# First mixer of a four-layer block: decay differences and key products written for GpSimd, and a new order on VectorE and ScalarE

## The reference

```python
xc = silu(causal_depthwise_conv(x))            # x: 16 sequences, 512 tokens, 256 wide
q, kg, v, g = xc @ wq, xc @ wkg, xc @ wv, xc @ wg + bg
gk = log_sigmoid(kg) / 16                      # decay of each key dimension
k = 1 - exp(gk)
# 8 heads, 16 key and 32 value dimensions each; over the tokens:
S = S * exp(gk_t)[..., None] + k_t[..., None] * v_t[..., None, :]
o_t = einsum('bhk,bhkv->bhv', q_t * scale, S)
o = o + sigmoid(einsum('bhld,hd,bhld->bhl', q, aug, k)[..., None] * v)
o = (o - mean(o)) * rsqrt(var(o) + eps)        # over a head's 32 values
x = layernorm(x + (silu(g) * o) @ wout)
```

## Time and profile before

| | us |
|---|---|
| three runs | 4456.34, 4467.64, 4469.37 |
| median | 4467.64 |
| profiled execution | 4455.1 |
| its span | 4453.5 |

### The profile page before, as it was taken

One profiled execution on the slowest core, in us unless ns is written; L12 is line 12 of the kernel. 1 busy time (PEld: TensorE's weight loads), 2 busy tenths in 40 slices (PEclk: granted clock), 3 DMA queues, 4 the chain that ended last, 5 costly groups with the idle time before them and its releaser, 6 DMA issues. The chain is left out here.

```text
span 4453.5 us, 69246 instructions
## 1 busy us (share of the span) xinstructions
PE 3941.6 (89%) x23860; PEld 3041.0 (68%) x23860; DVE 2464.7 (55%) x5456; ACT 1990.0 (45%) x4069; POOL 1195.6 (27%) x1878
## 2 busy tenths in 40 slices
PE   6888788598999999995689999989999999779998
PEld 3555555377888888884477777777777777656665
DVE  6888888452222222223667777777777777431111
ACT  5666665111222112221466666666666666432221
POOL 0111111101212221212344444444444443300000
PEclk8899899699999999997799999999999999889999
DMA  1010010254555555553111111111111111011111
GB/s 35 30 44 30 30 44 21 66 148 163 187 187 186 180 180 186 186 188 103 37 39 44 43 44 44 44 44 44 44 44 44 44 44 25 21 62 57 57 57 47
DMA packets 199445, 347.09 MB, mean 78 GB/s; under 512 B 75396, under 2 KB 150404, under 8 KB 180996
## 3 DMA queue, kind: packets, MB, share of 16 engines
q1 hardware_dynamic: 169284, 271.16, 18.8%
q0 software_dynamic: 29904, 72.65, 5.6%
HBM read 276.61 MB, written 68.16 MB: 77 GB/s over the span
## 5 line engine op out<-in xcount | busy, mean ns | idle before, releaser
L525 ACT ACTIVATE moe_rel<-moe_fc 128x512 f32<-128x512 f32 x284 | 169.6, 597 | 798.3 <-PE moe_fc L490 798.3
L490 PE MATMUL moe_fc<-moe_xT,moe_win 128*128 128x256 f32 x2272 | 503.6, 380 | 1.5 <-issue 0.8
L501 PE MATMUL moe_o<-moe_wout,moe_hT 128*128 128x256 f32 x2272 | 502.0, 379 | 0.0
L490 PEld LDWEIGHTS moe_fc<-moe_xT,moe_win 128*128 128x128 f32 x2272 | 432.6, 190 | 61.1 <-issue 2.1
L501 PEld LDWEIGHTS moe_o<-moe_wout,moe_hT 128*128 128x128 f32 x2272 | 426.3, 190 | 55.1
L549 DVE TENSOR_TENSOR moe_hT<-moe_rel 128x512 f32<-128x512 f32 x284 | 196.6, 692 | 360.7 <-ACT moe_rel L525 360.7
L1743 DVE SCALAR_TENSOR_TENSOR gdr_y<-gdr_bank,gdr_cw,gdr_y 128x511 f32<-128x511 f32 (+2 forms) x384 | 287.3, 748 | 41.4 <-ACT gdr_y L2053 27.0
L2330 PE MATMUL gdr_bank<-gdr_hT,gdr_wqkv 128*128 128x512 f32 x512 | 279.2, 678 | 29.6 <-ACT gdr_qk L2068 24.5
L558 DVE COPY moe_osb<-moe_o 128x512 f32<-128x512 f32 x71 | 49.1, 691 | 424.9 <-PE moe_o L501 424.9
L1305 PE MATMUL gdr_bank<-gdr_hT,gdr_wqkv 128*128 128x512 f32 x512 | 225.3, 598 | 3.6 <-ACT gdr_hT L1323 3.6
L1338 DVE TENSOR_TENSOR gdr_kb<-gdr_bank,gdr_x 128x512 f32<-128x512 f32 x32 | 20.6, 686 | 366.4 <-PE gdr_bank L1314 366.4
(11 more groups left out here) (393 smaller groups left out, 8804.2 us busy)
## 6 DMA issues: line engine op xcount, KB each, us to landing
moe_win<-in_moe_w SPq DMA_DIRECT2D x71, 1024.0 KB, 7.6
moe_wout<-in_moe_w SPq DMA_DIRECT2D x71, 1024.0 KB, 5.2
slots_out<-moe_osb POOLq DMA_DIRECT2D x71, 256.0 KB, 7.3
gdr_fz<-mixed_rows SPq DMA_DIRECT2D x18, 512.0 KB, 3.8
gla_xp<-in_xT_rows SPq DMA_DIRECT2D x16, 512.0 KB, 4.4
gla_xres<-in_x_rows SPq DMA_DIRECT2D x16, 512.0 KB, 3.8
token_rows<-gla_x POOLq DMA_DIRECT2D x16, 512.0 KB, 3.4
rt_W<-in_fc_b SPq DMA_DIRECT2D x32, 256.0 KB, 3.4
```

Of the source, the lines that this page charges most:

```text
L490: ins = nc.tensor.matmul(fc_ps[j][:, m % 2, :], win[u][:, c, m * P:(m + 1) * P], xT[:, c, :], start=(c == 0), stop=(c == DT - 1))
L501: ins = nc.tensor.matmul(o_ps[u][:, t, :], hT[u][:, k, t * P:(t + 1) * P], wout[u][:, k, :], start=(k == 0), stop=(k == FT - 1))
L525: nc.scalar.activation(rel[:, j, :, :], fc_ps[j][:], ACT.Relu).then_inc(relu_done, 1)
```

## The change

DVE no longer makes kt: GpSimd makes the eight differences as soon as G is there, ACT takes their exponentials as before, and GpSimd multiplies by k. GpSimd's loop gets the same `body` as the other engines: pow for rstd of b - 1, differences and products of b + 1, then the layer norm's pow and the two stores of b - 1. A new semaphore `Dk` counts GpSimd's differences, `G` the scan; the scan now waits until GpSimd has read the last G.

On DVE the calls of a body stand in a new order: variance and the product with gs (head norm 1 and 2) come first, `on` (3) ahead of the third masked scores, the gates behind them; the residual sum z (tail 0) comes right behind the fourth masked scores, the first convolution behind z and ahead of `products`; the layer norm's statistics, x1 and the logits are four parts now; the head means (0) are taken in the body that makes o. On ACT the squares move along to the end of the body, and the turned `on` is copied ahead of the exponentials. PE's and SP's code is unchanged.

```diff
+                def differences(b, u):
+                    wait, _ = waiter(pool, b)
+                    wait("G", 1)
+                    if later(b, 1):
+                        pool.wait_ge(s["sc"], (b - 1) * TT)
+                    for a in range(NSUB):
+                        n, r = SUB * (a + 1), SUB * a + SUB // 2 - 1
+                        nc.gpsimd.tensor_tensor(kt[u][:, :, a, 0:n], G[:, :, r:r + 1].broadcast_to([P, NCH, n]), G[:, :, 0:n],
+                                                ALU.subtract).then_inc(s["Dk"], 1)
+
+                def products(b, u):
+                    wait, _ = waiter(pool, b)
+                    wait("k", 1)
+                    for a in range(NSUB):
+                        n = SUB * (a + 1)
+                        wait("E", 5 + a)
+                        nc.gpsimd.tensor_tensor(kt[u][:, :, a, 0:n], kt[u][:, :, a, 0:n], k_[:, :, 0:n], ALU.mult).then_inc(s["kt"], 1)
...
+                def body(b, u, past, more, far):
+                    w = 1 - u
+                    if past is not None:
+                        head_rstd(past)
+                        if later(past, 0):
+                            logits_kept(past - 1)
+                    if more:
+                        differences(b + 1, w)
+                        products(b + 1, w)
+                    if past is not None:
+                        rows_out(past)
...
-                        for a in range(4 * (part - 1), 4 * part):
-                            n, r = SUB * (a + 1), SUB * a + SUB // 2 - 1
-                            done("D", 3 + a, tt(kt[u][:, :, a, 0:n], G[:, :, r:r + 1].broadcast_to([P, NCH, n]), G[:, :, 0:n], ALU.subtract))
...
-                        for a in range(4 * (part - 1), 4 * part):
-                            n = SUB * (a + 1)
-                            wait("E", 5 + a)
-                            done("kt", a + 1, tt(kt[u][:, :, a, 0:n], kt[u][:, :, a, 0:n], k_[:, :, 0:n], ALU.mult))
...
+                    if later(b, 0):
+                        dve.wait_ge(s["Dk"], b * NSUB)
+                    done("G", 1, v.tensor_tensor_scan(flat(G[:]), flat(notstart[:]), g[:], 0.0, ALU.mult, ALU.add))
```

More of the change, by code:

```diff
@@ L737, in _, with logits_kept @@
                     pool.nop().then_inc(x1_free, 1)
+                def logits_kept(b):
                     pool.wait_ge(lg_stored, b * 16 + 16)
                     pool.nop().then_inc(lg_free, 1)
+                def body(b, u, past, more, far):
[9 more added lines that the diff above has]
+                        rows_out(past)
+                starts(body)
+                for b in range(2, B - 2):
+                    body(b, b % 2, b - 1, True, b // 2 + 1)
+                ends(body)
+                logits_kept(B - 1)
             @block.vector
@@ L789, in products @@
-                def products(part, b, u):
-                    wait, done = waiter(dve, b)
[L791 to L801, removed]
-                        for a in range(4 * (part - 1), 4 * part):
-                            n = SUB * (a + 1)
-                            wait("E", 5 + a)
-                            done("kt", a + 1, tt(kt[u][:, :, a, 0:n], kt[u][:, :, a, 0:n], k_[:, :, 0:n], ALU.mult))
+                    ref8 = blocks8(G[:])[:, :, SUB // 2 - 1:SUB // 2].broadcast_to([P, NCH * NSUB, SUB])
@@ new lines, in differences, with products @@
+                    done("D", 1, tt(blocks8(eR[:]), blocks8(G[:]), ref8, ALU.subtract))
+                    done("D", 2, tt(khat[:], G[:, :, CH - 1:CH].broadcast_to([P, NCH, CH]), G[:], ALU.subtract))
+                def products(b, u):
+                    wait, done = waiter(dve, b)
+                    wait("q", 1)
+                    wait("E", 1)
+                    done("qt", 1, tt(qt[:], flat(eR[:]), qs[:], ALU.mult))
+                    wait("E", 2)
+                    done("qhat", 1, tt(qhat[u][:], flat(eG[:]), qs[:], ALU.mult))
+                    wait("k", 1)
+                    wait("E", 3)
+                    done("khat", 1, tt(khat[:], khat[:], k_[:], ALU.mult))
+                    done("aw", 1, tt(aw[:], qs[:], flat(k_[:]), ALU.mult))
@@ L888, in body @@
                     if recur:
[L889 to L899, removed]
                         outputs(1, b, u)
                     if more:
-                        products(0, b + 1, w)
+                        differences(b + 1)
+                    if recur:
+                        masked(3, b, u)
                     if past is not None:
                         tail(0, past)
+                    if far is not None:
+                        conv(0, b + 2, u, far)
                     if more:
-                        products(1, b + 1, w)
+                        products(b + 1, w)
                     if past is not None:
@@ L963, in exponents @@
                         done("E", 2, a_op(flat(eG[:]), flat(G[:]), ACT.Exp))
+                    elif part == 1:
                         wait("D", 2)
@@ L967, in exponents @@
                     else:
-                        for a in range(4 * (part - 1), 4 * part):
+                        for a in range(NSUB):
                             n = SUB * (a + 1)
-                            wait("D", 3 + a)
+                            wait("Dk", a + 1)
                             done("E", 5 + a, a_op(kt[u][:, :, a, 0:n], kt[u][:, :, a, 0:n], ACT.Exp))
@@ L1031, in body @@
                         silu(b + 2, u)
+                    if inside(b):
+                        squares(b, u)
                     if more:
```

53 lines of the change are left out of this document (24 added, 29 removed).

## The result

| kernel | median of the runs, us | ratio to before, 95% interval |
|---|---|---|
| before | 4462.13 (4 runs, 4456.34 to 4469.37) | |
| changed | 4498.14 (4 runs, 4495.4 to 4509.8) | 1.0085, 1.0058 to 1.0111 |

The change makes the kernel 36 us slower. The profiled execution took 4509.8 us, span 4508.2. The result is inside the forecast's range, but not by its likeliest case: that was +7.

A forecast was written before the change was run, and what follows sets the result against it. The prediction took a loop between PE and DVE in the first mixer as the bound: 46.0 plus 2.3 for clock gives 48.3 against 47.78 us a period, +7 over 14 periods, so 4474 us, range 4425 to 4510.

The forecast's parts named there:

- likeliest case: First mixer: values wait for ACT's copy, one values step at half clock; 48.3 us a period, +7 in all; chance 0.37.
- the rival with both values steps slow: PE at half clock through both values steps: 50.6 us a period, +39, 4507 us; chance 0.25.
- pow 6.49: GpSimd's pow for rstd, started just behind DVE's product, charged 6.49 us in every sequence instead of 5.45.
- G at 21.4: The gates' result G stands 21.4 us after o's fourth sum; before, 18.5 but with `on` still to come.
- GpSimd's kt: 16 added GpSimd operations per sequence take 12.6 us, end at about 39, and cost nothing if done before 46.
- x1 chain: DVE's products, statistics, o, second convolution and x1 after qt: x1 at 43.5, at the outside 45, so not limiting.
- From G to qt: DVE's work between G and qt takes 8.7 us, plus 2.3 of blocking, putting qt at 32.4.
- PE's wait at that turn: Sign of being right: PE's wait for `on`, 2.34 us before, nearly gone, with a new wait for ACT's values copy.
- the blocking: GpSimd's differences and products delay DVE's eR, khat, convolution and qt by 2.3 us together; bounds 0 and 4.6.
- the clock: PE at half clock for one values step after idle pauses, charged once as 2.3 us: 46.0 becomes 48.3.
- GpSimd yields: Rival: GpSimd runs only where DVE leaves the ports, DVE pays nothing; -39 to -71, about 4410 us; chance 0.07.
- the pow holds DVE too: Rival: pow keeps DVE's two-input operations out, `on` 1.4 later; 49.7 a period, +27, 4494 us; chance 0.03.

The follow-up runs named there:

- order alone: The changed kernel with kt's eight differences and eight products back on DVE instead of GpSimd; 4506.6 us, ratio 1.0104.
- the new one: Against the changed kernel, DVE order with gates and o*gs inside the wait for rstd, qt early: 4366.6 us with kt on GpSimd, 4451.6 on DVE.
- one-column kt: The changed kernel with GpSimd's kt operations cut to one column: 4450.1 us; gates also right behind on: 4449.0; PE's pause filled as well: 4400.1.

## Why the prediction held its range and was 29 us short

That 4498 lies inside the range owes something to luck. The likeliest case alone was given 4455 to 4490; the top of the range came from the rival with both values steps slow (4507), and that was not the cause.

Step by step, offsets from o's fourth sum:
- *Right.* Variance forecast at 8.5, measured at 8.53 (566.78); DVE's wait for rstd 2.3 (2.43); pow 6.49 (6.48) and G at 21.4 (21.41). From qt on as well: 5.7 to the first values copy (593.53 to 599.26: 5.73), 7.3 for the last two values steps with one at half clock (599.31 to 606.59: 7.28), 2.9 from the start of x1's turn to the next o (2.89). PE's two pauses come to 5.26 ("more than 5"). GpSimd's kt is 14.3 us, forecast 12.6 without blocking, and ends 36.4 behind o (39 forecast), far from its limit. The x1 chain did not bind.
- *The step that failed:* "From G to qt DVE has o 0.46, eR and khat 1.45, fourth masked scores 1.74, z 1.45 …: 8.7". It counts work only, because PE was taken to be there first ("PE itself got there some 2 earlier"). PE was late: its turn also waits for the gates' first step, and its scores then ran at half clock. One of the prediction's own signs failed with it: PE's wait at that turn was to be nearly gone, and went from 2.34 to 4.09. DVE waits 0.20 + 0.38 + 0.96 + 1.01 = 2.55 us there. With that, qt stands at 35.3 instead of 32.4, and the 2.9 go through to the period: 48.3 + 2.9 = 51.2. The code had it: `on` and `gq` both stand in PE's `tail`, and only the first was followed.
- *Mis-sized:* the blocking, 2.3, measured 2.74 (eR 0.11, khat 0.20, convolution 1.62, qt 0.81).
- *Right value, wrong weight:* the clock was charged as a fixed 2.3 on one step. The runs show it as what ties the parts together: saving 2.4 ahead of qt gave nothing until PE's pause was filled.
- The rivals. Both steps slow happened, but only in some periods; it was not the cause. "GpSimd yields" and "the pow holds DVE too" are out by the rows above. The Trainium skill (SBUF — State Buffer, "SBUF: two separate sides") has the shared port pair locked for a whole instruction. kt's products bear that out (0.69 became 1.50); the pow doesn't, since a product of 1.23 ran at its own length inside 5.45.

What costs the 36 us is then: the order, which puts z, a wait for PE and a convolution ahead of qt (order alone +47, qt moved ahead of the convolution some -37 to -39 against the changed kernel). On that path blocking and clock are each paid in full: without either one, the time is back at 4450 or 4452. These sizes don't add, since each works through the same wait for the values copy. The move of kt itself is a gain, 28 us in the old order and 80 to 85 in the new one. Not separated: how much of the order's loss is qt's place and how much the late turn, other than in the runs with one-column kt.

## What to carry to other kernels

Read the waits of each instruction that a new order makes early, all of them: a bank that another engine still reads counts like a missing input. Then follow the moved work to the first copy that frees a bank (here qt, spread, values), and put nothing ahead of it that isn't needed there. And before a saved microsecond is counted, ask whether PE will only wait longer and come back at half clock.

## What the runs showed of the hardware

- GpSimd's and DVE's two-input operations take turns one by one: beside GpSimd's kt products three convolution steps took 3.37 to 4.20 instead of 2.33, and 2.35 when GpSimd's operations were cut to 8 elements a partition. In the changed kernel's profile each of the three, and qt, ended 0.55 us behind the end of a GpSimd product.
- A saving on the critical path can vanish whole in PE's clock: 47.80 us a period with 0.50 and 0.55 granted in two steps, 43.86 with 1.00 throughout, the difference being six matmul passes of 0.46 us that do nothing.
- What makes DVE wait beside GpSimd's differences and products did not hold it beside a `pow`: a DVE product kept its 1.23 inside a pow of 5.45 (128x32). The other way round, a DVE product that ran when the pow started made the pow 6.48.
